# Graph attention: masks of twice the width in one ring of three or four, accumulators round eight PSUM banks

## What is computed

```python
h = (x @ W).reshape(N, H, D)
el = jnp.einsum('nhd,hd->nh', h, al)
er = jnp.einsum('nhd,hd->nh', h, ar)
e = jax.nn.leaky_relu(el[src] + er[dst], NEG_SLOPE)
m = jax.ops.segment_max(e, dst, num_segments=N)
ex = jnp.exp(e - m[dst])
s = jax.ops.segment_sum(ex, dst, num_segments=N)
alpha = ex / s[dst]
out = jax.ops.segment_sum(alpha[:, :, None] * h[src], dst, num_segments=N)
```

## Time and profile before

| | us |
|---|---|
| median of 3 runs | 2374.59 |
| lowest, highest | 2371.84, 2375.01 |
| span of the profiled execution | 2375.9 |
| PE busy over the span | 1749.6 (74%) |
| DVE busy | 1671.4 (70%) |
| ACT busy | 1385.3 (58%) |
| POOL busy | 334.5 (14%) |
| mask phase of the first attention layer, first ACT mask to last instruction | 344.4 (446.6 to 791.0) |
| the same of the second | 344.5 (916.7 to 1261.2) |
| the same of the third | 272.3 (2060.4 to 2332.7) |

### The profile page before, as it was taken

How to read it: one execution, slowest core, us unless ns; L and a number is a source line. 1 busy time by engine, 2 the same in 40 slices (tenths; PEclk the granted TensorE clock), 3 DMA queues, 4 the chain that set the end, 5 groups by cost and what they waited for, 6 DMA issues and landing times. The chain is left out here.

```text
span 2375.9 us, 66901 instructions
## 1 busy us (share of the span) xinstructions
PE 1749.6 (74%) x21978; PEld 1347.5 (57%) x21978; DVE 1671.4 (70%) x3910; ACT 1385.3 (58%) x2252; POOL 334.5 (14%) x547
## 2 busy tenths in 40 slices
PE   3998864488989334998891489994977984288981
PEld 1333323488888224888881356662546983288881
DVE  6988875799999658999997511113332256799997
ACT  0246762899999328999992412122122352599993
POOL 2465301666000012000000000000000000400000
PEclk9999987699999677999996799997997997699996
DMA  1000000100110000110101110000001010000002
GB/s 59 1 2 2 2 10 2 35 31 29 36 36 25 12 2 35 36 36 24 36 25 50 44 39 1 0 0 6 1 0 37 22 54 10 16 21 25 19 19 88
DMA packets 29717, 54.86 MB, mean 23 GB/s; under 512 B 10222, under 2 KB 20820, under 8 KB 29104
## 3 DMA queue, kind: packets, MB, share of 16 engines
q1 hardware_dynamic: 24608, 43.89, 5.6%
q0 software_dynamic: 4880, 7.80, 1.0%
HBM read 43.19 MB, written 8.49 MB: 22 GB/s over the span
## 5 line engine op out<-in xcount | busy, mean ns | idle before, releaser
L1117 PE MATMUL ps<-R,M 128*128 128x132 f16 (+1 forms) x8640 | 810.3, 221 | 268.1 <-DVE M L1030 151.6
L1117 PEld LDWEIGHTS ps<-R,M 128*128 128x128 f16 x8640 | 729.6, 97 | 311.5 <-issue 182.8
L986 ACT ACTIVATE Rm<-rows,cB 128x1280 bf16<-128x1280 f32 (+1 forms) x832 | 884.1, 1153 | 35.3 <-DMA rows<-rowd 17.6
L1125 PE MATMUL ps<-HB,C 128*128 128x66 f16 x6400 | 596.3, 193 | 0.0
L1030 DVE TENSOR_TENSOR M<-Rm,C 128x1280 f16<-128x1280 bf16 (+1 forms) x832 | 554.0, 688 | 54.3 <-ACT Rm L986 47.2
L1125 PEld LDWEIGHTS ps<-HB,C 128*128 128x128 f16 x6400 | 571.7, 97 | 0.0
L1389 PE MATMUL psA<-R,C 128*128 128x512 f16 (+1 forms) x1200 | 255.0, 352 | 96.7 <-POOL ones L1441 41.0
L546 DVE TENSOR_SCALAR ohc<-cells,near 128x1280 f16<-128x1280 f16 x387 | 212.9, 550 | 52.9 <-PE acc L571 49.3
L571 PE MATMUL acc<-ohc,ohl 128*128 128x420 f16 (+1 forms) x1161 | 244.2, 348 | 1.5 <-DVE ohl L548 0.2
L1389 PEld LDWEIGHTS psA<-R,C 128*128 (+1 forms) x1200 | 119.8, 100 | 194.5 <-issue 109.6
L1033 DVE SCALAR_TENSOR_TENSOR M<-rows,cN,C 128x1280 f16<-128x1280 f32 x128 | 197.7, 1545 | 0.0
(11 more groups left out here) (274 smaller groups left out, 2326.5 us busy)
## 6 DMA issues: line engine op xcount, KB each, us to landing
rows<-rowd SPq DMA_DIRECT2D x32, 640.0 KB, 3.9
rows<-rowd SPq DMA_DIRECT2D x16, 320.0 KB, 3.5
xd<-R SPq DMA_DIRECT2D x1, 2560.0 KB, 7.4
xr<-xd SPq DMA_DIRECT2D x20, 128.0 KB, 2.0
xd<-HB SPq DMA_DIRECT2D x1, 2560.0 KB, 9.4
xr<-xd POOLq DMA_DIRECT2D x1, 2560.0 KB, 10.8
R<-in_x SPq DMA_DIRECT2D x1, 2432.0 KB
R<-in_x POOLq DMA_DIRECT2D x1, 2432.0 KB, 10.2
```

The source lines that it names most:

```text
L986: a.activation(Rm[:, s % SG, :], rows[:, p % 2, :], ACT.Relu, bias=cB[:, ds(h + s * nh, 1)]).then_inc(s_R, 1)
L1117: m = pe.matmul(region(p % 2, r), lhsT, rhs, start=first, stop=True, skip_group_check=True)
L1125: m = pe.matmul(both[:, :, cw:2 * cw], C[:, s * NP + p * W + r * P:][:, 0:P], VP[:, s, :, ds(h * cw, cw)], start=False, stop=True, skip_gr ...
```

## The change

The mask phase is rewritten.

- PARTS is 1 unsplit and 2 split: masks of W = 2560 and W = 1280. There are 8 units in every layer, still of 20 steps, each with RG = 20 accumulator regions in NB = 7 banks (three regions to a bank).
- `Rm` is `M` under another type: ACT writes the slot, DVE takes the minimum in place. The ring has 3 slots unsplit and 4 split; `Mn` has a ring of 3. ACT now waits for PE (`slot_free`: the step 3, or 4, earlier), DVE for a slot of `Mn` likewise (`low_slot_free`). LEAD is 2 unsplit and 3 split.
- The accumulators go round one ring of 8 banks: bank j of unit q is number (7q + j) mod 8. PE waits at each bank's first matmul of a unit for DVE's `add` of the bank that used it before: none for bank 0, bank j-1 of the unit before for bank j.
- `add` runs bank by bank behind ACT's copies (`s_tl` counts banks). Unsplit, the sums are made in R, in the memory of the weights of the head that is done; `tl`, `q1`, `stash` and `unstash` are gone there. Split, `tl` holds 20 regions, and ACT waits for the `mean` of the unit before.
- `on_act` is 16 of 20 steps unsplit (s % 5 != 4). MORE_ON_ACT is gone.
- The rows of the first two units are fetched in the phase before. All loops of the mask phase are written out and `hold` is not used in it.

The diff, cut to its core:

```diff
+                PARTS = 2 if split else 1
+                UNITS = nh * PARTS
+                TP = NT // PARTS
+                W = TP * P
+                RG = TP * (2 if split else 1)
+                NB = (RG + 2) // 3
+                SLOTS, LOWS, LEAD = (4, 3, 3) if split else (3, 0, 2)
+                rows = hp.sb("rows", [P, 2, W], f32)
+                row_terms = rowd[0:RT, :].rearrange("(h p t) j -> p h (t j)", h=nh, p=PARTS)
...
+                    @block.sync
+                    def _(sp):
+                        for q in range(2):
+                            sp.dma_start(rows[:, q, :], row_terms[q % PARTS, q // PARTS:q // PARTS + 1, :].to_broadcast([P, W])
+                                         ).then_inc(s_rows, 16)
+                        sp.wait_ge(s_rows, 32)
...
-                PARTS = 4 if split else 2
-                TP = NT // PARTS
-                W = TP * P
-                RG = 10
-                NB = (RG + 2) // 3
-                SG = 5 if split else 4
-                LEAD = 7 if split else 4
...
+                    M = ph.sb("M", [P, SLOTS, W], f16)
+                    Rm = M[:, :, :].bitcast(bf16)
+                    Mn = ph.sb("Mn", [P, LOWS, W], f16) if split else None
+                    tl = ph.sb("tl", [P, RG, cw], f32) if split else None
...
+                    ps = ph.ps("ps", [P, 8, 4 * P])
...
+                    def region(q, r):
+                        at = (r % 3) * 2 * XW
+                        return ps[:, (q * NB + r // 3) % 8, at:at + 2 * XW]
...
+                    on_act = [s for s in range(NT) if split or s % 5 != 4]
+                    slot = lambda q, s: (q * NT + s) % SLOTS
+                    low_slot = lambda q, s: (q * len(TWO) + TWO.index(s)) % LOWS
+                    def slot_free(eng, q, s):
+                        if q * NT + s >= SLOTS:
+                            eng.wait_ge(s_P, q * NT + s - SLOTS + 1)
+                    def low_slot_free(eng, q, s):
+                        k = q * len(TWO) + TWO.index(s) - LOWS
+                        if k >= 0:
+                            eng.wait_ge(s_P, k // len(TWO) * NT + TWO[k % len(TWO)] + 1)
+                    def landed(eng, q):
+                        if q >= 2:
+                            eng.wait_ge(s_row[q % 2], q // 2 * 16)
...
+                    def sums(q):
+                        h = q // PARTS
+                        if split:
+                            return tl[:, :, :]
+                        return R[:, :].rearrange("p (t w c) -> p t w c", t=NT, w=2)[:, :, :, h * cw:(h + 1) * cw]
...
+                                if s in on_act:
+                                    slot_free(a, q, s)
+                                    h = q // PARTS
+                                    a.activation(Rm[:, slot(q, s), :], rows[:, q % 2, :], ACT.Relu,
+                                                 bias=cB[:, h + s * nh:h + s * nh + 1]).then_inc(s_R, 1)
+                        def evacuate(q):
+                            if split and q:
+                                a.wait_ge(s_mean, q)
+                            a.wait_ge(s_P, (q + 1) * NT)
+                            for j, r, n, part in banks(q, 1):
+                                a.activation(sums(q)[:, r:r + n], three(part), ACT.Copy, scale=1 / LO).then_inc(s_tl, 1)
+                        for q in range(UNITS):
+                            landed(a, q)
+                            steps(q, 0, LEAD)
+                            if q:
+                                evacuate(q - 1)
+                            steps(q, LEAD, NT)
+                        evacuate(UNITS - 1)
...
+                        def low_part(q, s):
+                            low_slot_free(v, q, s)
+                            v.wait_ge(s_cut, q * len(TWO) + TWO.index(s) + 1)
+                            p = q % PARTS
                             Cs = C[:, s * NP + p * W:s * NP + (p + 1) * W]
...
+                            v.tensor_tensor(Mn[:, low_slot(q, s), :], Cs, M[:, slot(q, s), :], ALU.subtract).then_inc(s_Mn, 1)
...
+                            x = sums(q)
+                            xu, xv = (x[:, 0:TP, :], x[:, TP:2 * TP, :]) if split else (x[:, :, 0, :], x[:, :, 1, :])
+                            o = xu[:, :, 0:dh]
+                            if split:
+                                o = HB[:, 0:NT * nh * cw].rearrange("p (t c) -> p t c", t=NT)[
+                                    :, p * TP:(p + 1) * TP, h * cw:h * cw + dh]
...
                             def add():
...
+                                for j, r, n, part in banks(q, 0):
+                                    v.wait_ge(s_tl, q * NB + j + 1)
+                                    v.tensor_tensor(x[:, r:r + n], three(part), x[:, r:r + n], ALU.add).then_inc(s_E, 1)
                             def scale():
...
+                                v.wait_ge(s_E, (q + 1) * NB)
                                 ch(v.tensor_tensor(xv, xv, factor(F2), ALU.mult))
...
+                                ch(v.tensor_tensor(xu, xu, factor(F1), ALU.mult))
...
+                                v.wait_ge(s_mean, q + 1)
...
+                                if s in ONE:
+                                    pe.wait_ge(s_M, q * len(ONE) + ONE.index(s) + 1)
+                                else:
+                                    pe.wait_ge(s_Mn, q * len(TWO) + TWO.index(s) + 1)
+                                for r in range(RG):
+                                    first = s == 0 and r % 3 == 0
+                                    if first and (q - 1) * NB + r // 3 > 0:
+                                        pe.wait_ge(s_E, (q - 1) * NB + r // 3)
+                                    side = r // TP
+                                    cols = slice((r % TP) * P, (r % TP + 1) * P)
+                                    lhsT = Mn[:, low_slot(q, s), cols] if side and s in TWO else M[:, slot(q, s), cols]
+                                    rhs = UV[:, s, :, ds(h * (2 * cw) + side * cw, XW)]
```

More of the change, by code:

```diff
@@ L37 @@
 SLOPE = 0.2
-MORE_ON_ACT = {(0, 7), (1, 11)}
 EPS = 1e-5
@@ L980, in _, with steps @@
                     @block.scalar
                     def _(a):
[L982 removed]
+                        def steps(q, s0, s1):
                             for s in range(s0, s1):
[L984 to L987 removed]
@@ L989, in evacuate @@
-                        def evacuate(h, p):
-                            q = h * PARTS + p
-                            hold(a, s_P, (q + 1) * NT + SG)
-                            hold(a, s_E, q + 2)
-                            for r, n, part in banks(p % 2, 1):
-                                ins = a.activation(tl[:, r:r + n, :], part, ACT.Copy, scale=1 / LO)
-                            ins.then_inc(s_tl, 1)
-                        def rest(h, p, before):
-                            if before:
-                                evacuate(*before)
-                            steps(h, p, LEAD, NT)
@@ L1078, in mean @@
                                 ch.wait()
[L1079 to L1099 removed]
+                                v.tensor_tensor(o, xu[:, :, 0:dh], rec[:, :].unsqueeze(2).to_broadcast([P, TP, dh]),
+                                                ALU.mult).then_inc(s_mean, 1)
+                                v.wait_ge(s_mean, q + 1)
+                            return [add, scale, both, weight, inverse, mean]
+                        for q in range(UNITS):
+                            landed(v, q)
+                            steps(q, 0, LEAD)
+                            steps(q, LEAD, NT, evacuation(q - 1) if q else [])
+                        for stage in evacuation(UNITS - 1):
                             stage()
```

172 lines of the change are left out of this document (45 added, 127 removed).

## The result

| | before | after |
|---|---|---|
| median of the runs | 2373.82 us (4 runs, 2371.84 to 2375.01) | 2574.44 us (4 runs, 2573.15 to 2578.36) |
| span of the profiled execution | 2375.9 us | 2576.6 us |
| mean granted clock of TensorE | 0.902 | 0.875 |

The changed kernel takes 1.0848 times as long, with an interval of 1.0832 to 1.0863. The forecast was 2560 us, in a range of 2500 to 2605.

The account below looks back on a forecast made before the run. ACT bounds the kernel before the change; after it, the unsplit slot cycle, with no engine full. Terms 144 + 21 + 34 - 13 = +186 us on a 2375.9 span give 2562, median 2560; range 2500 to 2605.

Parts of the forecast that it names:

- Widths: Lengths of wider instructions in mask phases: ACT's mask 2.44 us, is-greater mask 2.94, seven copies 1.5; as load, a gain.
- The ring, unsplit: Unsplit mask phases: three slots used by ACT, DVE and PE in turn make five steps 11.2 us, 44.8 a head.
- The bank ring and the order at a head's start: Unsplit head starts: PE waits for DVE's adds behind ACT's copies and mask; a head 51.5 us, phase +72, twice +144.
- T + 5.8: Unsplit head start: PE resumes 5.8 us after T, the end of its last step of the head before.
- PE's clock: TensorE's clock halves after stops at head and unit starts: 2 us a head, 0.8 a split unit, +34 (0 to +51).
- Split: Split layer's mask phase: shared slots and unit starts make a unit 36.1 us, the phase 293 against 272.3, +21.
- Rows and the rest: First rows fetched under the phase before: -13 us (-9 to -18); loops, register waits, `unstash`: 0 (0 to -6).
- Three phases save 4.7, 4.5 and 3.8: Fetching the first rows earlier saves these us at the three mask phases, -13 in all.
- Which rule applies: Mask phases: grouping helps a saturated engine, smaller instructions unsaturated ones holding up another; buffers keeping ACT full decides; no size.

## Why the prediction was right, step by step

**Widths.** Right: masks of 2.43 us (2.44 said), minimum 1.49, is-greater mask 2.88 (2.94), copies 1.65 for seven with the next mask after 1.47 (1.5), and adds 1.91.

**The ring, unsplit.** Right in size and cause. Five steps take 11.2 us as worked out. Shown by three runs at full width (431, 376 and 356 us for three, four and five slots) and two at half (368 and 344 for four and five).

**The bank ring and the order at a head's start.** Right: PE resumes at T + 5.84 for the T + 5.8 said. With the clock's 2 us a head was to be 53.5; the starts of the copies lie 52.5 to 54.2 us apart, 53.6 and 53.5 on average in the two layers. Two small errors cancel in this: without the clock's loss a head is 51.2 where 51.5 was said, and the loss is 2.3. The run with the adds first shows the order on DVE as the cause.

**PE's clock.** The sum of 34 measured 30 to 35 (30 by the two medians; 12.7, 13.8 and 8.3 by the phases, 35 in all), but not for the reasons given. The prediction knew one slow stretch for each stop. Unsplit that one costs 1.3 us, and the 2 us a head came out because a second one, of 1.4 us, follows in ten of 14 heads; that part is luck. Split it is 1.2 a unit and not 0.8. The stops are 5.57 us at 14 places (5.6 said) and 4.26 at seven (4.7 said).

**Split.** The term that was mis-sized. With its clock the phase was to be 293 + 5.6 = 299 and was 307. ACT's rows of one split unit in the changed kernel and in the one that keeps PE at work:

```profile
2302.07 1.59 ACT L1003 ACTIVATE tl<-ps 128x195 f32<-128x195 f32 x7
...
2339.80 1.59 ACT L1003 ACTIVATE tl<-ps 128x195 f32<-128x195 f32 x7
```

```profile
2276.14 1.60 ACT L1003 ACTIVATE tl<-ps 128x195 f32<-128x195 f32 x7
...
2312.45 1.60 ACT L1003 ACTIVATE tl<-ps 128x195 f32<-128x195 f32 x7
```

This unit is 36.3 us with the clock kept and 37.7 without, where 36.1 and 36.9 were said. So the chain of the unit was right to 0.2 us, and what was short is the clock: 1.4 for the 0.8 taken, 4 us over seven units. (Two of the seven still take 37.2 and 37.3 with PE kept at work, so the phases differ by 1.2 a unit.) A first unit of 34 where 36.8 passed makes 3, and the 0.2 a unit the rest.

**Rows and the rest.** The step "Three phases save 4.7, 4.5 and 3.8" failed in part: they saved 0.2, 1.0 and 5.2. The rows did land early; but their fetch was costed as if nothing but the phase before ran beside it, and in the first two layers DVE's wait for the all-reduce on the path there grew by 4.6 us each. It gave 7 to 11 us in place of 13. Loops, register waits and `unstash` at nothing have no run of their own; the unsplit phases leave about 1 us for them in all.

**Which rule applies.** In sentences that the rest does not need: of the two in the Trainium skill (Perfetto Trace Analysis, Optimizing Scalar/DVE Operations), the one on breaking up instructions where ScalarE and VectorE cause bubbles described the changed kernel, whose ACT is busy for 74%. The trace agrees, 344 us in five half slots for 431 in three whole ones, though it is the number of slots that does it: five whole ones with the adds first take 346. The one on grouping speaks of throughput in a saturated engine, and no run here reached that state with masks of 2560.

The sum fell short by 8 us in the split phase and 6 in the rows: 14 in all, the distance of 2560 from 2574. The unsplit phases, 417 and 14 of clock said, came out at 431, with the help of the two errors that cancel.

## What to carry to other kernels

When an instruction is made larger and its buffers fewer, work out the round of one slot through all engines, with whatever the engines do between, and compare it with the number of slots times the spacing of the producer. Saved overhead counts only while that round is shorter. And where accumulators are handed over in a ring, look at what stands ahead of the read-out in its engine's order: here seven adds moved ahead of one mask gave back 110 us. TensorE's clock is a part of that; filling the stops alone gave back 30.

## What the runs showed of the hardware that was not expected

- A large broadcast into SBUF can hold up GpSimd. In the first layer the all-reduce over the partitions began at 403.62 us with 2 x 1.28 MB of rows in flight and at 398.54 without; fetched just behind it, the rows put off GpSimd's next work from 10.3 to 12.5 us after the reduce; fetched behind that, both stand within 1 us of where they did. In the third layer, where DVE waits only 0.57 us for the reduce, 2 x 0.64 MB in flight delayed nothing. That a load of code for GpSimd shares the DMA engines with the rows would explain it, but no run isolates this, and the DMA record of neither kernel has a packet of the kind `instruction` between 385 and 415 us. The cause stays open. The Trainium skill (GPSIMD Engine Reference, Instruction dispatch) says that the first call of a freshly loaded kernel pays a load of its code of about 6 us, which the profile shows as no instruction; the 5.06 us that DVE waits for the reduce without rows in flight would fit, but no run here shows such a load.
- After 5.57 us without work TensorE's clock was at 0.50 from its first matmul on, for 5.5 us; after the 2.97 us stop it ran on at full clock for 1.2 us first. In ten of 14 heads it fell to 0.50 again some 12 us after the stop's end, around a wait of 2.0 to 2.4 us. Matmuls into an unused corner of an open bank, 68 short ones a head, raised the mean of the phase from 0.91 to 0.97 and were worth 30 us.
- Working in place cost DVE nothing: 817 ns for a minimum of 1280 columns in its own memory and 817 from ACT's ring into its own.
